# A Mamba and LoRA layer on one core: ScalarE takes B's rows out of PSUM, transposed tiles get two buffers, and the LoRA factor's product is made ahead of condition 1

## The chip, the cores and the metric

The kernel runs on 1 core of one Trainium2 chip. The metric is the device time of one execution in microseconds (us). An execution under the profiler is also taken; its span runs from the first to the last instruction. The engines are TensorE (PE; PEld is its weight load), VectorE (DVE), ScalarE (ACT), GpSimd (POOL) and SyncE (SP, which only issues DMAs here). Each works through its own instructions strictly in the order in which the program gives them.

## The reference

```python
# x: (32, 64, 1024) fp32
def cond(x, ids, W, A, B):            # LoRA of rank 16, adapter chosen per batch
    return x @ W + (x @ A[ids]) @ B[ids]
def attn(x, A_log, D, x_proj_w, dt_proj_w, dt_proj_b):      # selective scan, 16 states
    A = -exp(A_log)
    xp = x @ x_proj_w.T               # 32 columns dt_in, 16 columns B, 16 columns C
    dt = softplus(dt_in @ dt_proj_w.T + dt_proj_b)
    dA = exp(dt[..., None] * A)
    dBx = dt[..., None] * B[:, :, None, :] * x[..., None]
    h_t = dA_t * h_{t-1} + dBx_t      # over 64 steps; y_t = sum over n of h_t * C_t
    return y + D * x
x = x + attn(cond(x, ids1, W, A, B), ...)
x = x + ffn(cond2(x, ids2, ...), ...)  # a second LoRA layer, then 4 gated low-rank experts
```

## The kernel before

**Tiling.** The 32 batches are worked in 8 groups G of 4 (T = 256 tokens). The 1024 channels are 8 blocks j of 128 partitions. For each block the 16 states are worked in 4 units un (8 states of 2 batches: 1024 columns), so a group has 32 steps (j, un), the whole kernel 256. In each step

- TensorE makes dBx of the unit (`b_times_dtx`, 4 matmuls of `stacked` with the diagonal matrices `Bd`, into one of two PSUM tiles dBx0 and dBx1),
- VectorE runs the scan h = dA * h + dBx (line 1009), 1024 columns,
- GpSimd multiplies h by C into `hC` (line 578),
- TensorE, three steps later (LAG = 3), adds up the states by 8 transposing matmuls into yp[j % 2] (`sum_states`, line 1212),
- ScalarE makes dA, the exponentials of dt * A, for a later step (`decays`, line 612).

**Jobs.** All other work is put between the steps by a table written out by hand: `JOBS[(j, un)]` is a list of `job(name, i, bank, ks, ahead)`. FIRST, SIXTH and FINAL are the tables of group 0, of the last group but one and of the last; SIXTH is JOBS without the jobs for two groups on (xT, GAs, xr and the early parts of cond). The bank says which PSUM tile the job's product goes to: "A" is jb[0], "B" is jb[1], "Y" is yp[j % 2], which `sum_states` of block j writes from step (j, 3) on. Before TensorE writes a bank it waits until the bank's last tenant is released (`tenant`, `released`). TensorE does `b_times_dtx`, then `sum_states`, then the jobs of the step. VectorE does the jobs of a step after its scan; those in LATE_ON_DVE (dtz, cond and others), and on ScalarE those in LATE_ON_ACT (stack, Bst, xT, dtz and others), one step later.

The jobs around the change:

- `xT` i (0 to 3): x of a later group, transposed. ScalarE copies the high part (line 641), VectorE makes the low part (line 907).
- `GAs`, `xr`: the LoRA factor A split in high and low, and its product with xT (16 matmuls of 256 columns). VectorE masks it into `low` (line 911).
- `cond` i: 24 matmuls of W with xT for the channels of block i, then 1 with `low` and the LoRA factor B. Of the work ahead, cond 0 and the first eighth of cond 1 are made in the group before.
- `xproj`, then `dtz` i: dt before softplus; three operations of ScalarE (lines 593 to 597), one of VectorE (line 811), for blocks 2i and 2i + 1; dtz 4 and 5 are those of the next group.
- `Bst`: B's rows, transposed three times over onto 96 partitions (line 1145). Before, ScalarE makes the high part of rows 64 to 95 (line 660), VectorE writes the low part back to the same PSUM bank (line 921). From that bank VectorE makes the four diagonals `Bd` (`b_diagonals`, line 826), placed by `DIAGONALS`: 0, 1 and 2 at (7, 0), (7, 1), (7, 3) for the next group, 3 at (0, 1). The bank is released by the fourth. PE's `b_times_dtx` waits for its diagonal where j is 0.
- `stack` i: GpSimd multiplies dt by u into `dtx` (line 558, placed by `DTX`), TensorE transposes it, ScalarE makes the high half of `HL` (line 637), VectorE the low half (line 903), SP writes HL to HBM (`put_dtx`) and reads it back in another layout (`stack_dtx`) as `stacked`. stack 8 and 9 are blocks 0 and 1 of the next group. dtx and HL have one buffer each: GpSimd waits for the transpose before it, ScalarE for the DMA that reads HL.

`add_residual` (line 817) stands on VectorE before the scan at un = 3.

**Set-up.** Before group 0, W is split into high and low parts piece by piece: ScalarE `W_high(o)`, VectorE `W_low(o)` (line 949), and `put_W(o)` writes the pair to HBM. TensorE transposes xproj's and dtproj's weights, makes the first seven eighths of cond 0 and of cond 1, then xr, then the rest of both, then cond 2 to 7, xproj and what the first scan needs. ScalarE's order is: xprojT (line 703), dtprojT (lines 706, 709), GAs, put_W 0 and 1, W_high 2, put_W 2, W_high 3, put_W 3. VectorE's is: dtprojT (line 959), GAs, W_low 2, W_low 3, then `low`.

## Time and profile before

| | us |
|---|---|
| median of 3 runs | 902.66 (901.97 to 914.94) |
| the profiled execution | 902.51 |
| its span, first to last instruction | 900.7 |
| TensorE busy | 810.4 (90%) |
| VectorE busy | 761.5 (85%) |
| GpSimd busy | 661.1 (73%) |
| ScalarE busy | 639.3 (71%) |
| scans (line 1009), 256 | 582.7 |
| multiplications by C (line 578), 256 | 612.7 |
| mean granted clock of TensorE | 0.963 of full speed |

Busy time is an average over the stages. The granted clock has two levels, 1.0 (2.4 GHz) and 0.5 (1.2 GHz). A row of the timeline gives the start, the time from the first start to the last end of the instructions merged in it, their number, and in brackets how long the engine was idle before and what ended that. Matmuls of one engine overlap, so a row of TensorE may start before the row above it has ended.

### The profile page before, as it was taken

What the parts mean: (1) busy time and instruction counts of PE and PEld (TensorE: products, weight loads), DVE (VectorE), ACT (ScalarE), POOL (GpSimd) and SP (SyncE); (2) the same over time, 40 slices, a digit from 0 to 9 for tenths busy, and PEclk for the clock granted to TensorE, in tenths of its full rate; (3) what the DMA queues carried; (4) which work ended last, traced back from release to release, by engine and by line L of the source; (5) the groups of instructions that cost most, each with busy time, mean ns of one, the idle gap of its engine ahead of it and who ended that gap; (6) DMA issues with size and microseconds to landing.
All of it is one profiled execution on the core that took longest, in us unless ns stands there. A gap on an engine that the chain in (4) does not pass through costs nothing.

```text
span 900.7 us, 18606 instructions
## 1 busy us (share of the span) xinstructions
PE 810.4 (90%) x6416; PEld 773.0 (86%) x6416; DVE 761.5 (85%) x688; ACT 639.3 (71%) x1481; POOL 661.1 (73%) x349
## 2 busy tenths in 40 slices
PE   5898999899989999899989998899998999778884
PEld 4898999799978998799988997889988999677772
DVE  2437789988998899988999896998999979999993
ACT  4547677788776877777786875778777867779750
POOL 2004878689877888688877885779876978889891
PEclk9996999999999999899999998999999999899998
DMA  9988688375557557475666755476674744253221
GB/s 245 376 325 270 207 260 229 135 234 187 188 178 249 191 159 239 160 251 153 209 196 206 225 166 190 128 251 200 192 226 136 243 149 147 84 164 101 88 65 47
DMA packets 103113, 172.24 MB, mean 191 GB/s; under 512 B 21865, under 2 KB 71657, under 8 KB 94830
## 3 DMA queue, kind: packets, MB, share of 16 engines
q1 hardware_dynamic: 85614, 94.12, 35.0%
q10 hardware_dynamic: 17408, 76.95, 24.4%
q8 instruction: 53, 0.87, 0.4%
q14 instruction: 38, 0.31, 0.1%
HBM read 137.33 MB, written 33.69 MB: 190 GB/s over the span
## 4 chain that ended last, share of the span: by engine, by line
PE 60%; DVE 15%; ACT 8%; issue 6%; POOL 6%; DMA 3%; SPq 1%; ACTq 0%; POOLq 0%; DVEq 0%
PE jb L1045 26%; PE yp L1212 17%; DVE h L1009 10%; PE dBx L1045 8%; POOL hC L578 5%; ACT dA L612 3%; PE yp L1045 3%; PE jb L1049 3%; PE yp L1049 2%; DVE HL L903 1%; DVE Bd L826 1%; DMA x<-in_x 1%; DMA GA<-in_L_cond_lora_B_w 1%; PE yp L1217 1%; DMA stacked<-dtx_scratch 1%
## 5 line engine op out<-in xcount | busy, mean ns | idle before, releaser
L578 POOL TENSOR_TENSOR hC<-h,Cb 128x1024 f32<-128x1024 f32 (+1 forms) x256 | 612.7, 2395 | 161.2 <-DVE h L1009 144.8
L1009 DVE TENSOR_TENSOR_SCAN h<-dA,dBx 128x1024 f32<-128x1024 f32 x256 | 582.7, 2279 | 50.3 <-PE dBx L1045 40.4
L612 ACT ACTIVATE dA<-dt,negA 128x252 f32<-128x252 f32 x1024 | 430.3, 494 | 67.5 <-DVE h L1009 57.3
L1212 PE MATMUL yp<-ident,hC 128*128 128x128 f32 x2048 | 277.9, 280 | 27.7 <-DVE xT L907 11.3
L1212 PEld LDWEIGHTS yp<-ident,hC 128*128 128x128 f32 x2048 | 238.9, 145 | 33.6 <-issue 28.1
L1045 PE MATMUL jb<-xT,Wst 128*128 128x256 f32 x1416 | 213.9, 293 | 0.0
L1045 PE MATMUL dBx<-Bd,stacked 96*128 96x256 f32 x1024 | 187.6, 306 | 10.4 <-DVE h L1009 5.2
L1045 PEld LDWEIGHTS jb<-xT,Wst 128*128 128x128 f32 x1416 | 183.7, 192 | 1.9
L1045 PEld LDWEIGHTS dBx<-Bd,stacked 96*128 96x128 f32 x1024 | 147.5, 196 | 15.9 <-issue 12.8
L558 POOL TENSOR_TENSOR dtx<-dt,u 128x256 f32<-128x256 f32 x64 | 47.2, 738 | 44.4 <-DVE dt L811 42.4
L637 ACT ACTIVATE HL<-yp 128x256 fp32r<-128x256 f32 x54 | 20.4, 377 | 42.6 <-PE yp L1049 40.3
L647 ACT ACTIVATE u<-jb 128x512 f32<-128x512 f32 x31 | 18.6, 598 | 39.3 <-PE jb L1045 36.9
L1045 PE MATMUL jb<-low,GB 128*128 128x256 f32 x128 | 38.3, 380 | 2.3 <-DVE low L911 2.3
L1049 PE MATMUL yp<-ident,dtx 128*128 128x128 f32 x108 | 21.7, 284 | 18.9 <-DVE dt L811 11.7
L826 DVE TENSOR_TENSOR Bd<-jb,diag 96x1024 fp32r<-96x1024 f32 x32 | 38.2, 1197 | 0.1
L903 DVE TENSOR_TENSOR HL<-yp,HL 128x256 fp32r<-128x256 f32 x54 | 22.4, 414 | 16.7 <-ACT HL L637 16.5
L1217 PE MATMUL yp<-ident,Du 128*128 128x128 f32 x128 | 35.0, 274 | 0.0
L1045 PE MATMUL jb<-G,x1T 128*128 128x132 f32 x256 | 33.7, 279 | 1.0 <-ACT x1T L639 0.7
L1049 PEld LDWEIGHTS yp<-ident,dtx 128*128 128x128 f32 x108 | 13.5, 145 | 22.9 <-DVE dt L811 14.3
L639 ACT ACTIVATE x1T<-jb 128x512 f32<-128x512 f32 x32 | 19.0, 594 | 19.7 <-PE jb L1049 19.4
L1045 PEld LDWEIGHTS jb<-G,x1T 128*128 128x128 f32 x256 | 30.8, 190 | 1.8 <-ACT x1T L639 0.9
L603 ACT ACTIVATE Du<-u,Dsb 128x256 f32<-128x256 f32 x64 | 31.6, 495 | 0.0
(170 smaller groups left out, 729.4 us busy)
## 6 DMA issues: line engine op xcount, KB each, us to landing
...
```

Source lines behind the costliest of these rows:

```text
L558: pool.tensor_tensor(dtx[:, :], dt[:, i % NDT, :], u[:, i % K, :], ALU.mult).then_inc(dtx_made, 1)
L578: pool.tensor_tensor(*(x[:, :, ns, :] for x in times_C(un)), ALU.mult).then_inc(hC_made, 1)
L603: act.activation(Du[:, i % 4, :], u[:, i % K, :], ACT.Copy, scale=Dsb[:, i % K:i % K + 1]).then_inc(Du_made, 1)
L612: act.activation(dA[:, half % NDA, :].rearrange("p (b n t) -> p b n t", b=GB_, n=HS)[:, :, n, 1:STEPS], dt[:, j % NDT, :].rearrange("p (b ...
L637: act.activation(HL[:, 0, :, :].rearrange("p q d -> p (q d)"), psum[:, 0:2 * P], ACT.Copy).then_inc(hi_made, 1)
L826: dve.tensor_tensor(Bd[0:ROWS, NQ // 2 * p:NQ // 2 * (p + 1), HS * half:HS * (half + 1), :], rows[:, NQ // 2 * p:NQ // 2 * (p + 1), HS * h ...
L903: dve.tensor_tensor(HL[:, 1, :, :].rearrange("p q d -> p (q d)"), psum[:, 0:2 * P], HL[:, 0, :, :].bitcast(fp32).rearrange("p q d -> p (q ...
L1009: dve.tensor_tensor_scan(h[:, un % NH, :], dA[:, half % NDA, UNIT * p:UNIT * (p + 1)], dBx[un % 2][:, :], 0.0, ALU.mult, ALU.add).then_inc ...
L1045: return pe.matmul(o, lhsT, rhs, start=start, stop=stop, **kw)
L1049: return pe.matmul(o, in_, ident[first:first + n, first:first + n], is_transpose=True, start=True, stop=True)
L1212: last = pe.matmul(y, hC[:, un % NHC, P * n:P * (n + 1)], ident[:, :], is_transpose=True, start=un == 0 and n == 0, stop=False, skip_group ...
L1217: last = pe.matmul(y, Du[:, j % 4, P * p:P * (p + 1)], ident[:, :], is_transpose=True, start=False, stop=True, skip_group_check=True)
```

## The change

Tables: at (6, 2) Bst goes to "Y" and xT 3 to "B". stack 8 and 9 go to "B". The first three eighths of cond 0 move from (7, 0), where they stood ahead of stack 8, to (7, 1). Diagonal 0 of the next group moves from (7, 0) to (6, 3). FIRST gets the same edits.

Bst: ScalarE copies all 96 rows, rounded, into Bhl, and rows 64 to 95 once more, unrounded, into the new tile B_raw; that releases the bank. VectorE makes the low part from B_raw and Bhl, and the diagonals from Bhl, all in SBUF. Since diagonal 0 is now made before the group's last block has used the old one, b_diagonals waits for dBx_full.

Buffers: dtx and HL get two buffers, and what waited for the last use now waits for the last but one. The DMA scratch of GpSimd, which issues no DMA here, is cut to make room.

Set-up: on TensorE xr moves between the first parts of cond 0 and cond 1, to another PSUM bank; on ScalarE GAs, W_high 2, put_W 0 and 1 and W_high 3 move ahead of dtprojT; on VectorE GAs, W_low 2, W_low 3 and `low` do.

```diff
@@ JOBS and FIRST
-    (6, 2): [job("Bst", 0, "B"), job("xT", 3, "Y"), job("dtz", 4, "A")],
+    (6, 2): [job("Bst", 0, "Y"), job("xT", 3, "B"), job("dtz", 4, "A")],
     (6, 3): [],
-    (7, 0): [job("xr", 0, "Y", (0, 4)), job("xr", 0, "Y", (4, 8)), job("cond", 0, "A", (0, 3), 2), job("stack", 8, "Y")],
-    (7, 1): [job("cond", 0, "A", (3, 4), 2), job("dtz", 5, "Y")],
-    (7, 2): [job("cond", 0, "A", (4, 8), 2), job("stack", 9, "Y")],
+    (7, 0): [job("xr", 0, "Y", (0, 4)), job("xr", 0, "Y", (4, 8)), job("stack", 8, "B")],
+    (7, 1): [job("cond", 0, "A", (0, 4), 2), job("dtz", 5, "Y")],
+    (7, 2): [job("cond", 0, "A", (4, 8), 2), job("stack", 9, "B")],
@@
-DIAGONALS = {(0, 1): 3, (7, 0): 0, (7, 1): 1, (7, 3): 2}
+DIAGONALS = {(0, 1): 3, (6, 3): 0, (7, 1): 1, (7, 3): 2}
@@ buffers
+        B_raw = sb("B_raw", [P, NQ, R])
-        dtx = sb("dtx", [P, T])
+        dtx = sb("dtx", [P, 2, T])
-        HL = sb("HL", [P, 2, 2, P], fr)
+        HL = sb("HL", [P, 2, 2, 2, P], fr)
@@ GpSimd, make_dtx
-                wait(pool, full["stack"], K * G + i)
+                wait(pool, full["stack"], K * G + i - 1)
@@ ScalarE, stack
-                    wait(act, HL_out, 16 * (K * g + i))
+                    wait(act, HL_out, 16 * (K * g + i - 1))
@@ ScalarE, Bst
-                    wait(act, b_step, 2 * g)
-                    act.activation(Bhl[2 * Q:ROWS, :, :]..., psum[2 * Q:ROWS, 0:NQ * R], ACT.Copy).then_inc(b_step, 1)
+                    wait(act, Bd_made, UNITS * g)
+                    wait(act, b_low, g)
+                    act.activation(Bhl[0:ROWS, :, :]..., psum[0:ROWS, 0:NQ * R], ACT.Copy).then_inc(b_rows, 1)
+                    act.activation(B_raw[2 * Q:ROWS, :, :]..., psum[2 * Q:ROWS, 0:NQ * R], ACT.Copy).then_inc(b_rows, 1)
@@ ScalarE, set-up
+            job("GAs", 0, 0, None)
+            W_high(2)
+            put_W(0)
+            put_W(1)
+            W_high(3)
             for i in range(2):
                 ...
-            job("GAs", 0, 0, None)
-            put_W(0)
-            put_W(1)
-            W_high(2)
             put_W(2)
-            W_high(3)
             put_W(3)
@@ VectorE, b_diagonals
-                dve.wait_ge(b_step, 2 * G + 2)
+                dve.wait_ge(b_low, G + 1)
+                if G:
+                    dve.wait_ge(dBx_full, UNITS * (K * G - 1) + un + 1)
@@ VectorE, Bst
-                    low_rows = psum[2 * Q:ROWS, 0:NQ * R]
-                    dve.tensor_tensor(low_rows, low_rows, Bhl[2 * Q:ROWS, :, :]..., ALU.subtract).then_inc(b_step, 1)
+                    low_rows = Bhl[2 * Q:ROWS, :, :]
+                    dve.tensor_tensor(low_rows, B_raw[2 * Q:ROWS, :, :], low_rows.bitcast(fp32), ALU.subtract).then_inc(b_low, 1)
@@ VectorE, set-up
+            job("GAs", 0, 0, 0, None)
+            W_low(2)
+            W_low(3)
+            job("xr", 0, 0, 0, set_bank(3))
             for i in range(2):
                 ...
-            job("GAs", 0, 0, 0, None)
-            W_low(2)
-            W_low(3)
-            job("xr", 0, 0, 0, set_bank(4))
@@ TensorE, released
                 if name == "Bst":
-                    return Bd_made, UNITS * g + UNITS
+                    return b_rows, 2 * g + 2
@@ TensorE, set-up
             job("cond", 0, 0, 0, jb[0], "A", (0, K - 1))
             pe.wait_ge(taken["xT"], 4)
+            job("xr", 0, 0, 0, set_bank(3), None)
             job("cond", 1, 0, 0, jb[1], "B", (0, K - 1))
             wait(pe, set_taken, 1)
-            job("xr", 0, 0, 0, set_bank(4), None)
@@
-    nc = _bacc.Bacc("TRN2", target_bir_lowering=False, num_devices=1)
+    nc = _bacc.Bacc("TRN2", target_bir_lowering=False, num_devices=1, dynamic_dma_scratch_size=1024)
```

## Rows read from the trace of the kernel before

**Rows 1.** Busy time by stage, cut at scan starts; the first line names the columns.

```profile
core 0: us, PE busy (x) PEld busy (x) DVE busy (x) ACT busy (x) POOL busy (x), PEclk, DMA share, GB/s
72.20:180.18 107.98, 101.72 (x785) 99.49 (x785) 90.32 (x68) 77.19 (x182) 81.23 (x40) 0.92 0.71 221
384.41:464.50 80.09, 78.77 (x656) 75.92 (x654) 72.52 (x66) 61.43 (x145) 66.28 (x33) 1.00 0.63 205
464.50:487.07 22.57, 18.37 (x138) 17.62 (x139) 20.50 (x20) 15.96 (x38) 15.99 (x9) 0.92 0.54 170
773.25:794.40 21.15, 13.79 (x84) 12.87 (x83) 19.70 (x18) 16.10 (x38) 16.47 (x9) 0.76 0.31 97
```

**Rows 2.** Timeline, VectorE in group 3's boundary: start, us, engine, operation, idle before.

```profile
468.08 2.28 DVE L1009 TENSOR_TENSOR_SCAN h<-dA,dBx 128x1024 f32<-128x1024 f32 x1
470.28 0.67 DVE L811 SCALAR_TENSOR_TENSOR dt<-jb,dt 128x512 f32<-128x512 f32 x1
470.86 2.28 DVE L1009 TENSOR_TENSOR_SCAN h<-dA,dBx 128x1024 f32<-128x1024 f32 x1
473.05 1.19 DVE L826 TENSOR_TENSOR Bd<-jb,diag 96x1024 fp32r<-96x1024 f32 x1
...
475.64 0.42 DVE L903 TENSOR_TENSOR HL<-yp,HL 128x256 fp32r<-128x256 f32 x1 [1.06 <-ACT HL L637]
475.98 2.28 DVE L1009 TENSOR_TENSOR_SCAN h<-dA,dBx 128x1024 f32<-128x1024 f32 x1
...
483.09 0.42 DVE L903 TENSOR_TENSOR HL<-yp,HL 128x256 fp32r<-128x256 f32 x1 [0.94 <-ACT HL L637]
```

**Rows 3.** Timeline, TensorE in the same boundary.

```profile
464.64 0.75 PE L1049 MATMUL yp<-ident,xin 128*128 128x128 f32 x4 [0.30 <-DVE xT L907]
...
467.98 1.07 PE L1212 MATMUL yp<-ident,hC 128*128 128x128 f32 x8 [1.88 <-DVE xT L907]
...
471.04 2.84 PE L1045 MATMUL yp<-xT,GAs 128*128 128x256 f32 x16
...
474.80 0.38 PE L1049 MATMUL yp<-ident,dtx 128*128 128x128 f32 x2
...
482.20 0.44 PE L1049 MATMUL yp<-ident,dtx 128*128 128x128 f32 x2 [1.63 <-DVE dt L811]
...
483.66 1.06 PE L1212 MATMUL yp<-ident,hC 128*128 128x128 f32 x8 [0.56 <-DVE HL L903]
```

**Rows 4.** Timeline, TensorE's stack 8 in group 1's boundary.

```profile
269.26 0.44 PE L1049 MATMUL yp<-ident,dtx 128*128 128x128 f32 x2 [1.24 <-DVE low L911]
```

**Rows 5.** Timeline of the set-up, TensorE and ScalarE.

```profile
17.73 7.13 PE L1045 MATMUL jb<-xT,Bd 128*128 128x256 f32 x42 [1.10 <-DVE Bd L949]
...
18.29 0.60 ACT L703 ACTIVATE xprojT<-dBx 128x512 f32<-128x512 f32 x1 [1.00 <-issue]
...
25.14 2.14 PE L1045 MATMUL dBx<-xT,GAs 128*128 128x256 f32 x16 [0.28 <-DVE GAs L896]
...
29.91 0.70 PE L1045 MATMUL jb<-low,GB 128*128 128x256 f32 x2 [2.27 <-DVE low L911]
```

**Rows 6.** Busy time by stage, the 3.41 us after the 1.88 us wait.

```profile
469.21:472.62 3.41, 3.41 (x18) 3.41 (x17) 3.41 (x3) 2.77 (x7) 2.21 (x2) 0.50 0.01 3
```

**Rows 7.** Set-up: a stage by busy time, and SP's first put_dtx in the timeline.

```profile
63.00:65.00 2.00, 2.00 (x21) 2.00 (x20) 0.96 (x2) 0.63 (x2) 0.58 (x1) 1.00 0.06 14
...
65.30 0.36 SPq L421 DMA_DIRECT2D dtx_scratch<-HL  x1
```

**Rows 8.** Timeline, VectorE: 512 elements from PSUM, and from SBUF.

```profile
467.14 0.69 DVE L907 TENSOR_TENSOR xT<-yp,xT 128x512 fp32r<-128x512 f32 x1
...
17.50 0.68 DVE L949 TENSOR_TENSOR Bd<-Cb,Bd 128x512 fp32r<-128x512 f32 x1
```

**Rows 9.** Timeline of the boundary, ScalarE's copy of Bst and GpSimd's dtx 8.

```profile
465.60 0.27 ACT L660 ACTIVATE Bhl<-jb 32x128 fp32r<-32x128 f32 x1
...
472.79 0.74 POOL L558 TENSOR_TENSOR dtx<-dt,u 128x256 f32<-128x256 f32 x1
```

More of the change, by code:

```diff
@@ L102 @@
     (6, 1): [job("xT", 2, "Y")],
-    (6, 2): [job("Bst", 0, "B"), job("xT", 3, "Y"), job("dtz", 4, "A")],
+    (6, 2): [job("Bst", 0, "Y"), job("xT", 3, "B"), job("dtz", 4, "A")],
     (6, 3): [],
-    (7, 0): [job("xr", 0, "Y", (0, 4)), job("xr", 0, "Y", (4, 8)), job("cond", 0, "A", (0, 3), 2), job("stack", 8, "Y")],
-    (7, 1): [job("cond", 0, "A", (3, 4), 2), job("dtz", 5, "Y")],
-    (7, 2): [job("cond", 0, "A", (4, 8), 2), job("stack", 9, "Y")],
+    (7, 0): [job("xr", 0, "Y", (0, 4)), job("xr", 0, "Y", (4, 8)), job("stack", 8, "B")],
+    (7, 1): [job("cond", 0, "A", (0, 4), 2), job("dtz", 5, "Y")],
+    (7, 2): [job("cond", 0, "A", (4, 8), 2), job("stack", 9, "B")],
     (7, 3): [job("cond", 1, "A", (0, 1), 2)],
@@ L122 @@
 DU = {(0, 1): 2, (1, 3): 3, (2, 3): 4, (3, 1): 5, (4, 0): 6, (5, 0): 7, (6, 3): 8, (7, 1): 9}
-BANK_OF_B = next(q[2] for at in JOBS for q in JOBS[at] if q[0] == "Bst")
 LORA_A, LORA2, LORA_B, LORA2_B = range(4)
 ADAPTERS = {(1, 2): LORA2_B, (3, 0): 0, (4, 0): 1, (5, 2): 2}
-DIAGONALS = {(0, 1): 3, (7, 0): 0, (7, 1): 1, (7, 3): 2}
+DIAGONALS = {(0, 1): 3, (6, 3): 0, (7, 1): 1, (7, 3): 2}
 def layer_kernel(nc, x, ids1, ids2, W, loraA, loraB, A_log, Dw, xproj_w, dtproj_w, dtproj_b,
@@ L269, in layer_kernel @@
         last_half = sem("last_half_of_hC")
[L270 removed]
+        bc_made, b_rows, b_low, Bd_made = map(sem, ["bc_made", "b_rows", "b_low", "Bd_made"])
         gate_step, gate_exp, gm_hi, expB_put, expB_hi = map(sem, ["gate_step", "gate_exp", "gm_hi", "expB_put", "expB_hi"])
@@ L556, in make_dtx @@
                 pool.wait_ge(taken["dtz"], K // 2 * G + i // 2 + 1)
-                wait(pool, full["stack"], K * G + i)
-                pool.tensor_tensor(dtx[:, :], dt[:, i % NDT, :], u[:, i % K, :], ALU.mult).then_inc(dtx_made, 1)
+                wait(pool, full["stack"], K * G + i - 1)
+                pool.tensor_tensor(dtx[:, i % 2, :], dt[:, i % NDT, :], u[:, i % K, :], ALU.mult).then_inc(dtx_made, 1)
             pool.wait_ge(s_expB, 64)
@@ L658, in job @@
                 elif name == "Bst":
-                    wait(act, b_step, 2 * g)
-                    act.activation(Bhl[2 * Q:ROWS, :, :].rearrange("p q n -> p (q n)"), psum[2 * Q:ROWS, 0:NQ * R], ACT.Copy).then_inc(b_step, 1)
+                    wait(act, Bd_made, UNITS * g)
+                    wait(act, b_low, g)
+                    act.activation(Bhl[0:ROWS, :, :].rearrange("p q n -> p (q n)"), psum[0:ROWS, 0:NQ * R], ACT.Copy).then_inc(b_rows, 1)
+                    act.activation(B_raw[2 * Q:ROWS, :, :].rearrange("p q n -> p (q n)"), psum[2 * Q:ROWS, 0:NQ * R], ACT.Copy).then_inc(b_rows, 1)
                 elif name == "A2T":
@@ L820, in b_diagonals @@
             def b_diagonals(G, un):
-                dve.wait_ge(b_step, 2 * G + 2)
+                dve.wait_ge(b_low, G + 1)
+                if G:
+                    dve.wait_ge(dBx_full, UNITS * (K * G - 1) + un + 1)
                 half, p = un // 2, un % 2
                 of = [ROWS, NQ // 2, HS, Q]
-                rows = jb["AB".index(BANK_OF_B) if G else 0][0:ROWS, 0:NQ * R].rearrange("p (q n) -> p q n", q=NQ)
                 dve.tensor_tensor(
                     Bd[0:ROWS, NQ // 2 * p:NQ // 2 * (p + 1), HS * half:HS * (half + 1), :],
-                    rows[:, NQ // 2 * p:NQ // 2 * (p + 1), HS * half:HS * (half + 1)].unsqueeze(3).to_broadcast(of),
+                    Bhl[0:ROWS, NQ // 2 * p:NQ // 2 * (p + 1), HS * half:HS * (half + 1)].bitcast(fp32).unsqueeze(3).to_broadcast(of),
                     diag[0:ROWS, :].unsqueeze(1).unsqueeze(1).to_broadcast(of), ALU.mult).then_inc(Bd_made, 1)
@@ L902, in job @@
                     dve.wait_ge(hi_made, K * g + i + 1)
-                    dve.tensor_tensor(HL[:, 1, :, :].rearrange("p q d -> p (q d)"), psum[:, 0:2 * P],
-                                      HL[:, 0, :, :].bitcast(fp32).rearrange("p q d -> p (q d)"), ALU.subtract).then_inc(taken[name], 1)
+                    dve.tensor_tensor(HL[:, i % 2, 1, :, :].rearrange("p q d -> p (q d)"), psum[:, 0:2 * P],
+                                      HL[:, i % 2, 0, :, :].bitcast(fp32).rearrange("p q d -> p (q d)"), ALU.subtract).then_inc(taken[name], 1)
                 elif name == "xT":
@@ L1010, in body @@
                                                0.0, ALU.mult, ALU.add).then_inc(h_made, 1)
-                        if j == K - 1 and (j, un) in DIAGONALS and not final:
+                        if j >= K - 2 and (j, un) in DIAGONALS and not final:
                             b_diagonals(G + 1, DIAGONALS[j, un])
@@ L1100, in job @@
                     for a in range(2):
-                        last = tr(psum[:, P * a:P * (a + 1)], dtx[:, P * a:P * (a + 1)], P)
+                        last = tr(psum[:, P * a:P * (a + 1)], dtx[:, i % 2, P * a:P * (a + 1)], P)
                 elif name == "x1T":
@@ L1258, in _ @@
                         for a in range(4):
-                            last = tr(set_bank(3 + i)[:, n * a:n * (a + 1)], F_n[:, :].rearrange("m (p k) -> m k p", k=K)[:, 4 * i + a, :], n)
+                            last = tr(set_bank(4 - i)[:, n * a:n * (a + 1)], F_n[:, :].rearrange("m (p k) -> m k p", k=K)[:, 4 * i + a, :], n)
                         last.then_inc(set_full, 1)
```

11 lines of the change are left out of this document (4 added, 7 removed).

## The prediction

> **What bounds the kernel now.** I read the profile in four steps.
>
> First, the busy time by stage, cut at the starts of scans [rows 1]. The kernel is 72.2 us of set-up, eight groups of 32 scans and a tail. Group 0 takes 108.0 us, group 3 takes 80.09 + 22.57 = 102.7. Group 3 splits in two. In its body, from its first scan to scan (6,2), TensorE is busy 78.77 of 80.09 us: the body runs at TensorE's pace. In what I call the boundary, from scan (6,2) to the next group's first scan, TensorE is busy 18.37 of 22.57 us and VectorE 20.50: no engine is full, something waits. The change works in this stretch and in the set-up.
>
> Second, the timeline of VectorE and TensorE through that boundary [rows 2, 3]. TensorE waits four times: 1.88 us for DVE's low part of xT 3, because sum_states(6,0) writes yp[0], which xT 3 holds; 1.63 for DVE's dt, because stack 9 goes to yp[1], held by dtz 5; 0.56 for the low part of stack 9, before sum_states(7,0); 0.30 for xT 2. VectorE waits twice, each time for ScalarE's half of HL: 1.06 and 0.94 us. Stack 8 is late because the first cond 0 matmuls and xr stand ahead of it; it also shares yp[1] with xr, and in group 1, where TensorE's clock was full, it waits 1.24 for DVE's low of xr [rows 4].
>
> Third, the set-up [rows 5]. xr stands behind the first parts of both cond 0 and cond 1, and TensorE then waits 2.27 us for low (plus 0.28 before xr), because VectorE makes two pieces of W first. From there to the first scan TensorE and the chain of small operations have hardly a gap.
>
> Fourth, the granted clock [rows 6]: 0.50 in the 3.41 us after the 1.88 wait, that is 1.2 GHz instead of 2.4. The 16 matmuls of xr took 2.84 us there [rows 3] and 2.14 in the set-up at full clock [rows 5].
>
> **The change part by part.** The sum is made against the profiled execution, 902.51 us (span 900.7 and 1.8 around it); the median of the runs is 902.66, so the two may be used alike.
>
> *Set-up.* The first 42 matmuls of cond 0 and cond 1 take 7.13 us [rows 5], so after cond 0's 21 TensorE is at 17.73 + 3.57 = 21.3. xr needs GA_split. GAs now follows xprojT, whose copy ends at 18.9: 0.6 on ScalarE (a copy of that size) and 0.7 on VectorE [rows 5, 8], ready at 20.2. xr runs 21.3 to 23.45, cond 1 to 27.0. VectorE then makes W 2 and W 3 (two operations of 0.7 each, behind two copies of 0.6), low at about 24.2 to 24.6: before 27.0, so neither wait is left. Gain 0.28 + 2.27 = 2.55. dtprojT moves behind W 3 on ScalarE; nobody needs it before dtz 0, after the whole of cond. Of the DMAs on ScalarE's queue W_scratch 0 and 1 are issued 1.5 us earlier, 2 and 3 within a microsecond of before; their landing is awaited by W 5 to 7, a dozen microseconds later. W pieces 4 to 7 keep their distance to TensorE. What could eat the gain is the DMA, which moves the same bytes in either order: its share is 0.06 from 63 us on; put_dtx(0,0) was issued at 65.30, and would now go at 62.8, before that lull [rows 7]. On SP's queue nothing else changes place. I take 2.5, bounds 1.0 and 2.6. The F transposes swap two banks, at no cost.
>
> *Bst by ScalarE.* Added: ScalarE copies 96 rows instead of 32, and makes one more copy of 32. The copy of 32 rows and 128 columns took 0.27 [rows 9], one of 128 rows and 512 columns 0.60 [rows 5]: 0.27 to 0.60 each, and I take 0.27, so 0.27 more per group, ahead of xT 3's copy on an engine busy 15.96 of 22.57 us [rows 1]. dtz 4 follows 0.3 to 0.45 later, still ahead of VectorE. VectorE's low part and the four diagonals (1.19 each [rows 2]) read SBUF instead of PSUM. The same operation on 512 elements takes 0.69 from PSUM and 0.68 from SBUF [rows 8], so I price that at nothing; bounds 0 and 0.1 each. The Trainium skill, page VectorE: DVE Perf Modes, section on the TRN2 errata, gives PSUM sources 62 cycles more fixed cost than SBUF ones. By it each diagonal is 0.065 us cheaper and the sum some 1.5 us lower; the rows do not show such a difference.
>
> *Banks at (6,2).* Bst now waits for xT 2 where xT 3 did: 0.75 us of wait instead of 0.30. xT 3 in jb[1] no longer holds yp[0]; sum_states(6,0) needs only ScalarE's two copies, at about 466.15. TensorE is there at 466.45 instead of 467.98. dBx(7,0) is done at 468, so the new wait of diagonal 0 (dBx_full) costs nothing: VectorE comes to it at 470.3.
>
> *(6,3) to (7,3) on VectorE.* From start to start [rows 2] a scan takes 2.2, a diagonal 1.12, dt 0.58, HL 0.34; low and residual, of HL's size, are taken like it. Scan (6,3) at 468.08 as before. Diagonal 0 now follows it, dt at 471.4, scan (7,0) at 472.0: 1.1 late. Stack 8 needs dtx 8, which GpSimd makes behind hC(6,3), at 472.79 to 473.53 as before [rows 9]; dt at 472.05 is in time. xr ends at about 470.9, cond 0's nine matmuls no longer stand in between, so TensorE idles 2.7 us to 473.55 and issues stack 8 then instead of 474.80. ScalarE's HL is done at 474.35, VectorE has low at 474.2 and HL at 474.5, with no wait: scan (7,1) at 474.85, was 475.98. Diagonal 1, scan (7,2) at 478.2 (TensorE's dBx for it, with 12 matmuls of cond ahead, full at 477.5). Stack 9 in jb[1] no longer waits for dtz 5: TensorE reaches it at 480.4, was 482.20. dt, HL (wait 0.15), residual, scan (7,3) at 481.9, diagonal 2, next group's first scan at 485.2, was 487.07. So the boundary costs VectorE's own 20.50 and 0.15: gain 1.9. The second buffers of dtx and HL are what lets stack 8 and 9 follow so closely; elsewhere I price them at nothing, since none of the waits above is for the old buffer. Of what queues behind the new waits: behind Bst on TensorE stand xT 3 and dtz 4, half a microsecond late with slack on both.
>
> *The body after it* is TensorE's, which reaches sum_states(7,0) at about 481.2 instead of 483.66, so it keeps the 1.9. Against that stands the clock: a 2.7 us gap is longer than the 1.88 that was followed by half clock, and TensorE's work from stack 8 to stack 9 (6.85 us) now lies on the path. One half-speed stretch there costs up to 1.7 us of TensorE, 0.9 of it past VectorE's slack. One boundary in three: 0.3 each. The present stretch is hidden: at full clock the same stack 8 waited 1.24 us instead [rows 4]. The choice is mine, between 0 and 1.7.
>
> Sum: 2.5 set-up; six boundaries by 1.9 - 0.3 = 1.6, that is 9.6; the last boundary (no xT, xr, cond) can give its idle VectorE time, 21.15 - 19.70 = 1.45 [rows 1], taken as 1.3. Together 13.4: 902.5 - 13.4 = **889**.
>
> The Trainium skill, page TensorE: Matmul & The Clock Gate, section What's actually happening, says that activity releases the throttle and idleness brings it back; this trace agrees (0.50 after the wait), and it is what speaks against a longer single gap.
>
> **The rivals.**
> (a) TensorE keeps more than VectorE's 1.9: it enters each group 2.4 us earlier and loses less to its slow stretch, and the body follows it. For: the body's 98%. Against: GpSimd, busy 66.28 + 15.99 = 82.3 us a group [rows 1], has to follow. 2.6 a boundary: 2.5 + 15.6 + 1.4 = 19.5, 883.
> (b) The boundary gives nothing: the wait for dtx 8 and one half-speed stretch in each boundary hold stack 9 at 482. For: the present gaps are already followed by a slow stretch [rows 6]. Only the set-up and 0.3 a boundary: 898.
> (c) Slower: the clock stays at 1.2 GHz over all of stack 8 to stack 9. 6.85 us of work then end at 480.4 + 3.4 = 483.8, 1.6 later than stack 9 now. It decides from more than one stretch of 3.4 us per boundary on. Longer stretches exist: group 0's mean granted clock is 0.92 [rows 1], that is 17 of its 108 us at 0.5. In every boundary: 902.5 - 2.5 + 6 x 1.6 = 909.6.
>
> **How the numbers follow.** The forecast 0.52, (a) 0.26, (b) 0.17, (c) 0.05. The forecast's own range is 885 to 894. The range to hold the time 8 times in 10 reaches into (a) and (b): 879 to 899, with the DMA bound of the set-up (1.5) and the price of half clock (up to 1.7 a boundary) inside it. 2% below the median is 884.6, about what a measurement of this kernel can tell from no change: (a) lies beyond it, the tip of the forecast too; faster 0.27, within 2% 0.70, slower 0.03.
>
> **What would show it.** Right: no wait over 1 us between xr and the F transposes in the set-up, first scan at 69.7; sum_states at (6,3) without a wait for xT; stack 8 waiting for GpSimd's dtx instead; HL's waits on VectorE gone; boundary 20.6 to 21. Wrong: first scan after 71; a boundary above 22; granted clock 0.5 between stack 8 and stack 9 in most groups; GpSimd's waits for scans shrinking in the body, which is rival (a).

## The result, and the profile after

The changed kernel takes 911.42 us (median of 4 runs, 908.23 to 912.86) where the kernel before took 902.32 beside it: ratio 1.0114, interval 1.0062 to 1.0166. The forecast was 889, 1.5% faster; it became 1.1% slower, outside the range of 879 to 899. A second series has 911.93 against 910.13 for the kernel before (ratio 1.0039, 0.9996 to 1.0081): the loss is between nothing and 1.7%, and the 13 us of gain are in neither series.

The profiled execution: 908.23 us, span 906.0. Stages cut as in [rows 1]; then a window of 3.40 us.

```profile
388.54:467.99 79.45, 76.13 (x628) 73.10 (x626) 72.33 (x67) 61.75 (x145) 68.10 (x33) 1.00 0.65 210
467.99:491.28 23.29, 19.60 (x154) 19.12 (x155) 20.58 (x20) 16.18 (x39) 17.85 (x9) 0.93 0.49 153
478.93:482.33 3.40, 3.40 (x19) 3.40 (x18) 3.40 (x3) 1.85 (x5) 2.74 (x3) 0.50 0.21 77
```

The boundary of group 3 takes 23.29 us (before 22.57, forecast 20.7), and the new thing in it is GpSimd: busy 17.85 us for the nine operations that took 15.99. The costliest groups of instructions say the same of the whole run:

```profile
L578 POOL TENSOR_TENSOR hC<-h,Cb 128x1024 f32<-128x1024 f32 (+1 forms) x256 | 632.5, 2475 | 145.0 <-DVE h L1011 130.6
L558 POOL TENSOR_TENSOR dtx<-dt,u 128x256 f32<-128x256 f32 x64 | 54.2, 847 | 39.2 <-DVE dt L813 39.2
L829 DVE TENSOR_TENSOR Bd<-Bhl,diag 96x1024 fp32r<-96x1024 f32 x32 | 38.6, 1208 | 0.1
L1051 PE MATMUL jb<-ident,dtx 128*128 128x128 f32 x48 | 9.7, 284 | 26.0 <-POOL dtx L558 26.0
```

Before, the 256 hC took 612.7 us (mean 2395 ns) and the 64 dtx 47.2 (738 ns). On GpSimd only dtx was edited, its buffer index and what it waits for, and GpSimd works 27 us longer. The diagonals themselves have not changed (1208 ns, before 1197). The timeline of the boundary on VectorE and GpSimd, to be held against [rows 2, 9]:

```profile
471.55 2.28 DVE L1011 TENSOR_TENSOR_SCAN h<-dA,dBx 128x1024 f32<-128x1024 f32 x1
473.74 1.19 DVE L829 TENSOR_TENSOR Bd<-Bhl,diag 96x1024 fp32r<-96x1024 f32 x1
474.86 0.68 DVE L813 SCALAR_TENSOR_TENSOR dt<-jb,dt 128x512 f32<-128x512 f32 x1
475.46 2.27 DVE L1011 TENSOR_TENSOR_SCAN h<-dA,dBx 128x1024 f32<-128x1024 f32 x1
477.65 0.40 DVE L914 TENSOR_TENSOR low<-yp,own_batch 128x256 f32<-128x256 f32 x1
478.83 0.42 DVE L906 TENSOR_TENSOR HL<-jb,HL 128x256 fp32r<-128x256 f32 x1 [0.79 <-ACT HL L637]
...
473.91 3.24 POOL L578 TENSOR_TENSOR hC<-h,Cb 128x1024 f32<-128x1024 f32 x1 [1.06 <-DVE h L1011]
477.11 0.71 POOL L558 TENSOR_TENSOR dtx<-dt,u 128x256 f32<-128x256 f32 x1
...
495.99 1.73 POOL L558 TENSOR_TENSOR dtx<-dt,u 128x256 f32<-128x256 f32 x1
```

Diagonal 0 starts at 473.74, the hC beside it at 473.91, and that one takes 3.24 us instead of 2.4; dtx 8 waits behind it. In the next group's (0, 1), diagonal 3 starts at 495.94, just ahead of dtx 2, which takes 1.73 us instead of 0.74.

The last boundary takes 23.45 us, where it took 21.15. There Bst's low part, which now also reads two inputs from SBUF, started 0.02 us behind an hC and ended 0.15 us after it, having taken 2.53 us where it takes 0.28 in the other seven groups:

```profile
776.98 2.40 POOL L578 TENSOR_TENSOR hC<-h,Cb 128x1024 f32<-128x1024 f32 x1
777.00 2.53 DVE L924 TENSOR_TENSOR Bhl<-B_raw,Bhl 32x128 fp32r<-32x128 f32 x1 [0.23 <-ACT B_raw L662]
```

TensorE in the boundary of group 3, the counterpart of [rows 3]:

```profile
468.37 0.52 PE L1147 MATMUL yp<-ident,x1T 16*96 16x16 f32 x8 [1.03 <-DVE xT L910]
...
472.86 2.15 PE L1047 MATMUL yp<-xT,GAs 128*128 128x256 f32 x16
477.97 0.41 PE L1051 MATMUL jb<-ident,dtx 128*128 128x128 f32 x2 [2.96 <-POOL dtx L558]
478.14 0.72 PE L1047 MATMUL dBx<-Bd,stacked 96*128 96x256 f32 x4
478.70 1.69 PE L1214 MATMUL yp<-ident,hC 128*128 128x128 f32 x8
480.25 2.60 PE L1047 MATMUL jb<-xT,Wst 128*128 128x256 f32 x12
```

The 1.88 us wait for xT 3 is gone, as forecast, and one of 2.96 us for dtx 8 stands in its place. Behind it the clock is at 0.50: twelve matmuls of cond 0 take 2.60 us, which take 1.67 elsewhere.

### The profile page after: what moved, and what is told of

Its sections match the earlier page's. It is cut to its first block, busy times and chain, and to the rows that moved or that the text cites. A ratio compares the mean times of both kernels' runs of the same rounds, so it can differ in the third digit from the quotient of the medians.

```text
span 906.0 us, 18640 instructions
## 1 busy us (share of the span) xinstructions
PE 806.1 (89%) x6416; PEld 770.7 (85%) x6416; DVE 764.7 (84%) x688; ACT 643.4 (71%) x1489; POOL 688.2 (76%) x349
## 4 chain that ended last, share of the span: by engine, by line
PE 52%; POOL 12%; DVE 11%; issue 10%; ACT 9%; DMA 5%; SPq 0%; POOLq 0%; ACTq 0%; DVEq 0%
PE jb L1047 24%; PE yp L1214 13%; POOL hC L578 10%; PE dBx L1047 7%; DVE h L1011 6%; ACT dA L612 4%; PE jb L1051 3%; PE yp L1047 3%; DMA Cb<-c_scratch 2%; POOL dtx L558 2%; DMA dtx_scratch<-HL 1%; DVE Bd L829 1%; DMA x<-in_x 1%; PE yp L1051 1%; PE yp L1219 1%
## 5 line engine op out<-in xcount | busy, mean ns | idle before, releaser
L578 POOL TENSOR_TENSOR hC<-h,Cb 128x1024 f32<-128x1024 f32 (+1 forms) x256 | 632.5, 2475 | 145.0 <-DVE h L1011 130.6
L1214 PE MATMUL yp<-ident,hC 128*128 128x128 f32 x2048 | 274.7, 278 | 16.7 <-DVE HL L906 8.0
L1214 PEld LDWEIGHTS yp<-ident,hC 128*128 128x128 f32 x2048 | 236.7, 144 | 20.7 <-issue 11.4
L1047 PEld LDWEIGHTS jb<-xT,Wst 128*128 128x128 f32 x1416 | 186.2, 195 | 1.9
L558 POOL TENSOR_TENSOR dtx<-dt,u 128x256 f32<-128x256 f32 x64 | 54.2, 847 | 39.2 <-DVE dt L813 39.2
L829 DVE TENSOR_TENSOR Bd<-Bhl,diag 96x1024 fp32r<-96x1024 f32 x32 | 38.6, 1208 | 0.1
L910 DVE TENSOR_TENSOR xT<-jb,xT 128x512 fp32r<-128x512 f32 x26 | 17.8, 684 | 21.3 <-ACT xT L641 21.1
L639 ACT ACTIVATE x1T<-jb 128x512 f32<-128x512 f32 x32 | 19.1, 596 | 22.4 <-PE jb L1051 21.7
L641 ACT ACTIVATE xT<-jb 128x512 fp32r<-128x512 f32 x26 | 15.5, 596 | 26.8 <-PE jb L1051 26.2
L1051 PE MATMUL jb<-ident,dtx 128*128 128x128 f32 x48 | 9.7, 284 | 26.0 <-POOL dtx L558 26.0
L1047 PE MATMUL jb<-u,xprojT 128*128 128x256 f32 x128 | 30.5, 381 | 0.7 <-ACT u L647 0.7
```

The lines of the kernel that those rows point to most:

```text
L558: pool.tensor_tensor(dtx[:, i % 2, :], dt[:, i % NDT, :], u[:, i % K, :], ALU.mult).then_inc(dtx_made, 1)
L578: pool.tensor_tensor(*(x[:, :, ns, :] for x in times_C(un)), ALU.mult).then_inc(hC_made, 1)
L639: act.activation(x1T[:, 2 * i:2 * i + 2, :].rearrange("p k t -> p (k t)"), psum[:, :], ACT.Copy).then_inc(taken[name], 1)
L829: dve.tensor_tensor(Bd[0:ROWS, NQ // 2 * p:NQ // 2 * (p + 1), HS * half:HS * (half + 1), :], Bhl[0:ROWS, NQ // 2 * p:NQ // 2 * (p + 1), HS ...
L1047: return pe.matmul(o, lhsT, rhs, start=start, stop=stop, **kw)
L1051: return pe.matmul(o, in_, ident[first:first + n, first:first + n], is_transpose=True, start=True, stop=True)
```

## The experiments

Two causes are to be told apart, and each may have a share. **P**: a VectorE operation with two inputs in SBUF lengthens the GpSimd operation beside it. **C**: TensorE's wait for dtx 8 is followed by 1.2 GHz in a place where that counts. Each span is taken apart into the start of the first scan, the seven boundaries, the eight bodies and a tail of 36.0 us, the same in both. All ratios and intervals are against runs of the kernel before on the same chip. There it took 906.8 to 911.9 us, not the 902 from which the expected times were worked out, so it is the ratios that are compared.

| | first scan | sum of the boundaries | sum of the bodies | hC over 2.7 us |
|---|---|---|---|---|
| before | 72.2 | 156.4 | 636.1 | 7 |
| changed | 69.3 | 163.7 | 637.0 | 29 |

The sums of the bodies are not alike inside: before's hold some 6 us in group 4, where TensorE waits 3.2 us for a transfer of stacked. The shortest bodies take 78.7 us before, and 79.45 changed (three groups).

**Set-up alone.** The kernel before, with the hunks of the set-up only.

> The kernel before with the set-up part of the change alone. Theory P (the two engines GpSimd and VectorE hold each other up where both read SBUF) and theory C (TensorE's clock falls after the longer wait for dtx 8) both say that the loss lies in the boundary edits and not here: first scan at 69.3 us as in the changed kernel instead of 72.2, everything else as before, 899.5 us, ratio 0.997. A rival, that the moved set-up is what upsets the later phase of clock and DMAs, would give a time above before's, 905 or more.

906.93, ratio 0.9965 (0.9915 to 1.0015). First scan at 70.0; the boundaries take 156.5, as before. The set-up is not the cause.

**Old tables with the new copy of B, the masking left out, and condition 1 first.** Three edits of the changed kernel: the tables and diagonal 0 as before; the diagonals as an operation with one input; only the order in (7, 0) to (7, 1) as before.

```
-                    ... diag[0:ROWS, :].unsqueeze(1).unsqueeze(1).to_broadcast(of), ALU.mult)
+                dve.tensor_scalar(..., 1.0, None, ALU.mult)
```

> The changed kernel with the tables of before (banks, cond 0 ahead of stack 8, diagonal 0 at (7, 0)): what is left is the set-up, the second buffers, and Bst copied out by ScalarE with the diagonals read from SBUF. Theory P: each diagonal makes GpSimd's operation beside it about 0.9 us longer (3.24 instead of 2.37 us in the changed kernel), so GpSimd stays at 686 us busy instead of 661, and the time is 3 to 8 us above that of the set-up alone, 903 to 908. Theory C: the clock has nothing to do with it, TensorE's waits are those of before, and the time is that of the set-up alone, 899.5, with GpSimd at 661.

> The changed kernel, in which the diagonals are made as a copy of the same shape with one input from SBUF (times 1.0) instead of a product of two: the masking of Bd is left out, the rest is the same work. If the copy takes the same 1.2 us on VectorE, theory P says that GpSimd's operations beside it are 2.4 us again, its busy time 661, dtx 8 is 0.9 us earlier, the boundary of group 3 falls from 23.3 to about 21.5 to 22.5 and the time by 6 to 10 us to 902 to 905. Theory C says no change, 911, since the wait for dtx 8 stays over 2 us long.

> The changed kernel with the first three eighths of cond 0 back ahead of stack 8 in (7, 0). They fill TensorE's wait for dtx 8 (2.96 us in group 3) with 1.25 us of work. Theory C: the clock keeps 1.0 between stack 8 and stack 9, the 1.03 us wait of scan (7, 2) for dBx goes, the time falls by 6 x 1 to 2 us, to 900 to 905. Theory P: GpSimd's operations beside the diagonals stay 3.2 us, dtx 8 comes when it came, and the time falls by 3 us at most, to 908 or more.

910.48 (ratio 1.0017, 0.9969 to 1.0065), 898.0 (0.9940, 0.9895 to 0.9986) and 907.2 (0.9998, 0.9955 to 1.0040). With the old tables 29 hC over 2.7 us stay and the boundaries take 161.9 instead of the 156.5 of the set-up alone: the longer operations come with the copy of B, not with the table. In time the two kernels cannot be told apart, for their intervals overlap.

With condition 1 first the boundaries take 156.8, 6.9 less than changed, as C had it, and 29 hC stay long, as P had it; neither expectation holds whole, and three of the first six boundaries still have a half-clock stretch at (7, 0). (Its bodies sum to 646.2, but this profile is of the longest of its ten executions, 913.83 us, so nothing is read from that.)

The run with one input is not the clean control that it was meant to be, for that operation takes 0.66 us instead of 1.19, and hC beside it 2.71 to 2.78. Three of its seven boundaries take 20.65 to 20.71 us, the forecast's figure, but VectorE is busy only 18.98 us there instead of 20.5, so they are not the forecast's chain. What it does show is the price of half clock. The stages (boundary of group 3, of group 4, and a stretch of the latter):

```profile
460.14:480.80 20.66, 17.26 (x150) 16.99 (x151) 18.98 (x19) 15.63 (x37) 16.25 (x9) 1.00 0.46 125
563.76:585.98 22.22, 18.83 (x150) 18.56 (x151) 18.97 (x19) 15.61 (x37) 16.27 (x9) 0.92 0.43 139
573.75:577.15 3.40, 3.40 (x18) 3.40 (x18) 3.08 (x3) 2.27 (x6) 2.74 (x3) 0.50 0.21 77
```

The engines do the same work in both boundaries and TensorE waits 3.01 us for dtx 8 in both; only the second has the half-clock stretch, and it is 1.56 us longer. So such a wait is not always followed by half clock: of five boundaries of this run with the 3.01 us wait, three have the stretch.

**One operand back in PSUM.** The changed kernel; the second factor of each diagonal is read from dBx in PSUM instead of diag in SBUF (same shape, wrong factor from group 1 on). Beside it the same with condition 1 first, the changed kernel again, and one with dtz 4 and dtx 8 a step sooner.

```
-                    diag[0:ROWS, :].unsqueeze(1).unsqueeze(1).to_broadcast(of), ALU.mult)
+                    dBx[(s + 1) % 2][0:ROWS, :].rearrange("p (q n t) -> p q n t", ...), ALU.mult)
```

> The changed kernel, in which from group 1 on the second factor of the diagonals is read from PSUM (the next unit's dBx) instead of from diag in SBUF: the values of Bd are wrong, the operation, its shape and its 1.2 us are the same, and only one input lies in SBUF. Port theory: GpSimd's multiplications beside it are 2.4 us again (busy 663 instead of 688), dtx after diagonal 3 is 0.74 instead of 1.7 us, each boundary falls by 0.9 us at least to 22.4 where the clock still falls and to 20.7 to 21 where it does not; time 6 to 9 us below the changed kernel's. If two inputs in SBUF are not what matters (but the longer chain, or the clock alone), GpSimd stays at 688 and nothing moves.

> Both suspected causes taken away: the second factor from PSUM as in the run before, and the first three eighths of cond 0 back ahead of stack 8, to fill the wait for dtx 8. If port and clock together are the whole loss, most boundaries are 20.7 to 21.2 us, the forecast's, no boundary is above 22.5, and the time is 12 to 16 us below the changed kernel's, about 889 to 893 where before takes 902. If something else is lost as well, boundaries stay above 22.

> The changed kernel itself beside the next three on one chip. Both theories take its boundary of 23.3 us as 20.7 as forecast, 0.9 for GpSimd's longer operation ahead of dtx 8 (port) and 1.6 for TensorE at half clock afterwards. Expected: boundaries of 23.3 us again, 28 or 29 of GpSimd's multiplications over 2.7 us, one slow stretch after nearly every wait for dtx 8, time 5 us above before's.

> The changed kernel with dtz 4 moved from (6, 2) to (6, 1), behind xT 2, and dtx 8 made by GpSimd after hC(6, 2) instead of hC(6, 3). dtx 8 is then done some 3 us before TensorE comes to stack 8, so its wait of 3 us and the slow stretch after it should go (clock theory: boundaries of 20.6 to 21.5 us, time 10 to 14 us below the changed kernel's). The diagonals still read two inputs from SBUF: GpSimd's busy time stays at 688 (port theory), but ahead of dtx 8 it costs nothing now. If the longer operations of GpSimd hold up the scans themselves, boundaries stay at 22 or more.

897.06 (0.9876, 0.9795 to 0.9958), 898.72 (0.9846, 0.9762 to 0.9930), 911.93, and 907.74 (0.9979, 0.9932 to 1.0025). Where one operand lies changes 15 us, more than the 6 to 9 expected. GpSimd is busy 664.4 us instead of 688.2, and 7 hC are over 2.7 us as before the change. Two lines of its profile page, then a diagonal and the hC beside it, 0.16 us behind it as in the changed kernel:

```profile
PE 804.2 (90%) x6416; PEld 767.4 (86%) x6416; DVE 762.7 (86%) x688; ACT 641.6 (72%) x1489; POOL 664.4 (75%) x349
...
L834 DVE TENSOR_TENSOR Bd<-Bhl,dBx 96x1024 fp32r<-96x1024 f32 x28 | 33.7, 1203 | 13.0 <-PE dBx L1052 13.0
```
```profile
276.33 1.19 DVE L834 TENSOR_TENSOR Bd<-Bhl,dBx 96x1024 fp32r<-96x1024 f32 x1
276.49 2.43 POOL L578 TENSOR_TENSOR hC<-h,Cb 128x1024 f32<-128x1024 f32 x1 [1.05 <-PE yp L1219]
```

P is shown: same operation, same duration, same moment, and hC takes 2.43 us instead of 3.24 to 3.31. The boundaries of this run take 21.2 and 21.4 us without a half-clock stretch at (7, 0) and 22.7 with one (behind waits for dtx 8 of 2.67 us; the waits of 1.42 and 1.79 had none), though its diagonals wait 13.0 us for dBx, which they did not before. The last takes 23.09, for the low part still reads two inputs from SBUF. With condition 1 first as well, four boundaries take 20.4 us, but three take 24 to 26, where none was expected above 22.5. The changed kernel again has 28 hC over 2.7 us and three boundaries of 23.3, others from 22.3 to 24.6; it lies 1.8 us above before's median there, where 5 were expected.

The kernel before had the effect too. All of its seven hC over 2.7 us start 0.16 us behind a VectorE operation with two inputs in SBUF:

```profile
447.26 0.67 DVE L896 TENSOR_TENSOR GAs<-GA,GAs 128x512 fp32r<-128x512 f32 x1
447.42 2.75 POOL L578 TENSOR_TENSOR hC<-h,Cb 128x1024 f32<-128x1024 f32 x1 [0.37 <-DVE h L1009]
```

In the last run dtx 8 starts at 474.60 and TensorE finds it ready, with no half-clock stretch at (7, 0), yet the boundaries take 22.4 us, where C expected 20.6 to 21.5. For the move pushed Bst's low part beside an hC, and there is the same effect the other way round:

```profile
472.28 2.38 POOL L578 TENSOR_TENSOR hC<-h,Cb 128x1024 f32<-128x1024 f32 x1 [0.64 <-DVE h L1011]
473.17 1.64 DVE L924 TENSOR_TENSOR Bhl<-B_raw,Bhl 32x128 fp32r<-32x128 f32 x1 [0.38 <-ACT B_raw L662]
```

VectorE's operation takes 0.28 us elsewhere; here it starts inside an hC and ends 0.15 us after it. It does so in each of the first six boundaries, and scan (6, 3) starts 5.84 us after scan (6, 2) instead of 3.56; of these 2.3 us the low part's delay is 1.4, the rest dt, which now stands ahead of it, and the 0.38 us wait.

**B's rows kept in PSUM, with the rest of the change but one swap.** Bst goes to the last 128 columns of jb[1], whose first 256 take stack 8 and 9, and stays there, so diagonals and low part read PSUM. For that xT 3 goes to yp[0] again, as before the change. Then the same with 12 matmuls of no use ahead of stack 8, the same with condition 1 first, and the changed kernel with 20 such matmuls.

```
+        def b_in(g):
+            return jb[1][:, 512 - NQ * R:512] if g else jb[0][:, 0:NQ * R]
...
+                    if i == K:
+                        for k in range(FILLERS):
+                            mm(psum[:, 0:T], GAs[...], xT[:, 0, k % K, :], True, True)
                     pe.wait_ge(dtx_made, K * g + i + 1)
```

> The changed kernel with B's rows left in PSUM as before (in the last 128 columns of the bank that LoRA's products 8 and 9 use in their first 256, instead of being copied out by ScalarE), so that each diagonal has one operand in PSUM again. Set-up, two buffers of HL and dtx, stack 8 ahead of condition 1 and diagonal 0 at (6, 3) stay as changed. Nothing is left out. Theory P (a VectorE operation with two inputs in SBUF lengthens the GpSimd operation beside it by 0.9 us): GpSimd busy 664 us instead of 688, no hC over 2.7 us in the boundaries, boundaries of 21.2 us without and 22.7 with a half-clock stretch (23.3 in the changed kernel), the stretch (0, 0) to (6, 2) 78.6 us instead of 79.5, in all as the run with the other factor in PSUM: ratio 0.985 to 0.991, 897 to 902 us. Rival (the 15 us came from Bst leaving its bank and ScalarE's copy, or from the values of Bd that the run with the other factor had wrong): ratio 1.00 or more.

> g1_rows_kept, and 12 matmuls of no use (128x256, into the bank of LoRA's product 8, overwritten by it) put into TensorE's wait for dtx 8, which was 1.8 us in the run with the other factor in PSUM. Nothing is left out. Theory C (TensorE's wait is what the half-clock stretch at (7, 0) follows): the stretches at (7, 0) go in most of the seven boundaries, these take 21.2 us instead of 22.7, five of 1.5 us make 7.5 us: ratio to before 0.977 to 0.984. Rival (the stretch comes whatever TensorE does there, from the busy share of the whole boundary or from a wait elsewhere such as the 1.04 us for xT at (6, 2)): stretches and boundaries as in g1_rows_kept, within 2 us of it.

> g1_rows_kept, and condition 1's first matmuls ahead of LoRA's product 8 in (7, 0), as before the change. Nothing is left out. If the order of these two is worth what the forecast had (TensorE idles while condition 1 could run): 2 us less in each boundary with stack 8 first, so this kernel 8 to 14 us slower than g1_rows_kept. If it is worth nothing, as the runs with the other factor in PSUM have it (897.1 and 898.7 us): within 3 us of g1_rows_kept, four boundaries of 20.4 us and some of 24 to 26 with a half-clock stretch of 6.8 us in condition 1.

> The changed kernel, and 20 matmuls of no use (128x256, 2.8 us at full clock) in TensorE's wait for dtx 8, which is 3.0 us there. Nothing is left out. Theory C: half-clock stretches at (7, 0) go, boundaries of 21.7 us instead of 23.3, so 8 to 11 us less than the changed kernel: ratio to before 0.992 to 0.998. Rival (clock falls anyway, or the fillers run at half clock and hold stack 8 up): boundaries 23.3 or more, ratio 1.004 or more.

898.15 (0.9889, 0.9813 to 0.9966), 904.51 (0.9933, 0.9886 to 0.9980), 904.91 (0.9943, 0.9896 to 0.9991), 906.91 (0.9975, 0.9938 to 1.0012). The boundary of the first and a stretch of it, by busy time; then the timeline of its GpSimd and TensorE there:

```profile
461.61:482.62 21.01, 18.44 (x141) 17.82 (x142) 20.43 (x19) 16.08 (x38) 16.04 (x9) 0.92 0.52 138
464.59:467.99 3.40, 2.90 (x14) 2.93 (x15) 2.88 (x3) 3.19 (x9) 2.18 (x2) 0.50 0.44 148
```
```profile
467.55 2.40 POOL L580 TENSOR_TENSOR hC<-h,Cb 128x1024 f32<-128x1024 f32 x1 [1.22 <-DVE h L1012]
469.94 0.74 POOL L560 TENSOR_TENSOR dtx<-dt,u 128x256 f32<-128x256 f32 x1
470.83 0.41 PE L1052 MATMUL jb<-ident,dtx 128*128 128x128 f32 x2
```

Boundaries of 20.9 to 21.0 us (one of 23.2, with a wait of 3.29 us for a transfer of stacked; the last 20.4), near the forecast's 20.7 with VectorE's whole work, so its chain was about right without P. A half-clock stretch is in this one too, but right behind the wait for xT 3, which this kernel keeps, and there it costs 0.1 us: the boundary of group 4, which has none, takes 20.89. Stack 8 follows xr without a wait in the row above (only in group 4 does it wait, 1.37 us), so the fillers had no gap to fill: they ran 1.6 us, held stack 8 up by 1.4, and the boundaries take 22.4. Theory C's expectation for this kernel failed, for it rested on a wait that is not there. In the changed kernel, where the wait is, they did what C said; its boundary by busy time, and TensorE's timeline:

```profile
465.57:487.28 21.71, 20.32 (x173) 19.79 (x174) 20.49 (x19) 16.17 (x39) 17.91 (x9) 1.00 0.53 165
```
```profile
471.96 2.56 PE L1047 MATMUL jb<-xT,GAs 128*128 128x256 f32 x20
475.52 0.44 PE L1051 MATMUL jb<-ident,dtx 128*128 128x128 f32 x2 [1.01 <-POOL dtx L558]
```

In the first six boundaries no half-clock stretch is left at (7, 0); five of the six take 21.7 to 22.0 us (expected were 21.7) instead of 23.3. The sixth takes 23.97, with a wait of 3.82 us for a transfer of stacked at (7, 3); the last still takes 23.46, with its low part at 2.53 us. GpSimd's 17.91 us show that P is still there.

**Again, and the order alone.** The kernel with B's rows kept once more; and the kernel before with only stack 8 ahead of cond 0.

```
-    (7, 0): [..., job("cond", 0, "A", (0, 3), 2), job("stack", 8, "Y")],
+    (7, 0): [..., job("stack", 8, "Y"), job("cond", 0, "A", (0, 3), 2)],
```

> g1_rows_kept once more, with more rounds: its four runs had a median of 898.2 us and a ratio of 0.981 to 0.997, while the same kernel with condition 1 first had 904.9 us in ten runs. Theory P: boundaries of 21.0 us where no half-clock stretch lies behind (7, 0), six times 1.5 us less than before, 3 us less in the set-up and nothing elsewhere: ratio 0.985 to 0.991. Rival (the four runs were lucky ones, and the gain is that of the set-up with half of the boundaries' lost again in the groups' other steps): 0.993 to 0.997.

> The kernel before, and of the change only the order of two entries of the table: LoRA's product 8 ahead of condition 1's first matmuls in (7, 0), still in the bank that it had. Nothing is left out. Theory O (the order is what the forecast had the gain from: 1.2 us of product 8, given back to scan (7, 1)): boundaries of 21.3 us instead of 22.57, 7 us in all, ratio 0.990 to 0.994. Theory B (the gain comes from the two buffers, the bank of product 8 and diagonal 0 at (6, 3), and the order is worth nothing, as boundaries of 21.0 us with product 8 first and 20.5 to 21.5 with condition 1 first have it): boundaries of 22.3 to 22.6 us, ratio 0.998 to 1.002.

895.75 (0.9807, 0.9747 to 0.9867; a little more than P's 0.985 to 0.991), and 908.33 (0.9952, 0.9909 to 0.9994). The order alone makes the boundary longer, 23.25 us, which neither theory had:

```profile
478.43 0.44 PE L1049 MATMUL yp<-ident,dtx 128*128 128x128 f32 x2 [2.33 <-DVE low L911]
```

Stack 8 in yp[1] waits for low, and cond 0 stands behind it. With the new bank and buffers the order makes no difference to the boundaries (148.4 us in all with stack 8 first, 148.8 with condition 1 first). So the boundaries' gain comes from the bank of stack 8 and 9, the two buffers and diagonal 0 at (6, 3) together; which of the three was not separated. In time, 904.91 us with condition 1 first lies 6.8 above the 898.15 beside it, between the two expectations, with overlapping intervals; what the order is worth elsewhere stays open. That the order alone still had a ratio just below 1 is not explained by its profile.

**Where the rest went.** The kept rows give 8.0 us in the boundaries, but GpSimd then waits in the next group's first steps for C's rows. GpSimd's wait for them in the second profile of the kept rows (us in total, times, longest), and the same row of the kernel before:

```profile
POOL hC L580 <- DMA Cb<-c_scratch: 16.5, 5, 4.0
```
```profile
POOL hC L578 <- DMA Cb<-c_scratch: 5.3, 4, 2.0
```

The last experiment puts the load of C's third part ahead of stack_dtx on SP's queue at (7, 3); beside it the kept rows a third time.

```
+                        c_first = (j, un) == (K - 1, UNITS - 1) and not last
+                        if c_first:
+                            spread_c(G + 1, un - 1)
                         for name, i, g, gpar, psum in ended_before(G, par, j, un):
```

> g1_rows_kept, and on SP's queue at (7, 3) the load of C's third part ahead of the loads of LoRA's product 9 (stack_dtx), whose wait for the write of HL held it for 5 us. Nothing is left out. Theory: the boundary's gain is in part given back because GpSimd waits for C's rows in the next group's (0, 2) or (0, 3) (16.5 us in five waits in g1_rows_kept's second profile, 5.3 us in the kernel before), so issued 4 us sooner the third part lands before it is wanted and the fourth no later: the first four scans of a group take 11.3 to 12.5 us instead of 14.5 to 14.9, the whole group 1.1 us less, 7 times: ratio 0.970 to 0.982. Rival (the transfers share the DMA engines with those of product 9 and the bytes of the conditions' weights, so C's fourth part is as late as before, and product 9 later): as g1_rows_kept, within 2 us.

> g1_rows_kept a third time, on the chip of the run with C's rows sooner, to compare the two: ratio 0.981 to 0.989, the middle of its intervals so far.

893.59 (0.9854, 0.9815 to 0.9894) and 894.61 (0.9888, 0.9834 to 0.9942). The first four scans of groups 1, 2, 3 and 5 take 11.3 us as expected (14.1 to 14.9 in most groups without it), so in these steps the queue's order was the wait. GpSimd still waits 11.1 us for C's rows in all, where the three profiles of the kept rows have 14.1 to 21.1. The whole is 1 us shorter, which these runs cannot tell from nothing, and the ratio misses the expected 0.970 to 0.982: in its profile group 0 lost 7 us at another place and group 4 another 4.

## Why the prediction was wrong

**The set-up**: the waits were right, the size is not shown. xr follows cond 0 without a wait, and low is ready in time. The first profile has the first scan at 69.29 (forecast 69.7), a gain of 2.9. But that is in part the luck of two profiles: in the 16 profiles with the new set-up the first scan starts at 69.3 to 72.4 us, half of them below 70.3, and in the two with the old one at 72.20 and, in the run of the order alone, at 70.62. Its ratio alone, 0.9965, does not exclude 1.

**The low part and the diagonals from SBUF, priced at nothing**: this step failed, and with it "dtx 8 as before". The 0.69 against 0.68 of [rows 8] is true of VectorE's own time, and 1208 against 1197 ns confirms it. What was not asked is who else works then. Each diagonal starts just ahead of an operation of GpSimd, and each lengthens one: 22 hC by 0.9 us more than before, and seven dtx by 1.0 (one of them in the set-up). In the boundary that puts dtx 8 at 477.11, 5.56 us after the start of scan (6, 3), where it was 4.71. Its price is the step from the kept rows' 20.9 to 21.0 us to the 21.7 with fillers and no half clock, 0.7 to 0.8. In the body it is diagonal 3 beside dtx 2: 79.45 us in the shortest bodies where it was 78.7, an estimated 5 us over seven groups, which the forecast did not have at all. The kernel before already showed the effect, in the seven hC beside GAs, but only in GpSimd's rows.

The Trainium skill has the rule, page SBUF — State Buffer, section Who interferes with whom: a VectorE instruction with two SBUF inputs contends with a GpSimd instruction that reads SBUF, since its second input comes through the shared read interface. The runs agree: with one operand in PSUM the prolongation is gone. The Trainium skill, same page, section Summary: rules for kernel authors, says that the second to issue fully blocks until the first finishes. That agrees nearly: hC behind diagonal 0 would end at 474.93 + 2.38 = 477.31 by it, and ended at 477.15; the low part behind an hC ended 0.15 us after it.

**The price of half clock**: mis-sized. The forecast had 0.3 a boundary, from one in three. The changed kernel has one in five of the first six boundaries, starting 0.2 to 1.3 us after stack 8, behind waits of 2.96 to 3.56 us for dtx 8, and there it costs 1.56 (one input) to 1.6 (fillers). The sixth, that of group 1, waited 1.99 us and has none there; it takes 23.70 us with a wait of 3.53 at (7, 3). The forecast had 1.7 as a bound and let half of it vanish in VectorE's slack. Its observation that the old stretch is hidden was right, and it holds for the kept rows too. The kept rows' 20.9 to 21.0, with 0.7 to 0.8 for P and 1.6 for the clock, make the measured 23.3. That sum closes in part by construction, since P's and the clock's terms meet at the run with fillers; the independent check is the 1.56 of the run with one input.

**The VectorE chain**: about right. Boundaries of 20.9 to 21.0 with the kept rows, which do VectorE's whole work, stand against the forecast's 20.65. HL's waits are not gone in the changed kernel (0.79 at 478.83), since stack 8 is late.

**The wait for xT 3**: right; it is gone, and sum_states(6, 0) follows the dBx before it without one. Bst waits 1.03 us for xT 2 where 0.75 was forecast.

**The last boundary**: wrong, 23.45 instead of 19.85. It is the same cause at another operation: the low part takes 2.53 us instead of 0.28, and scan (6, 3) starts 5.40 us after scan (6, 2), where the kernel before has 2.97. The run with the other factor in PSUM, whose low part is as late, keeps 23.09; with the low part reading PSUM (the kept rows) it is 20.4.

**The rivals**: (c), 909.6, had the sign and nearly the size at a chance of 0.05, and the clock is half of its mechanism; but it wanted more than one stretch per boundary, and one suffices once GpSimd is late too. Rival (b) named the wait for dtx 8 with one stretch in each boundary, held to the old place of stack 9. No rival had GpSimd slower, which is the term that turned the sign. The gain of 13.4 us was not far off once the operand stays in PSUM (ratios 0.981 to 0.989 are 10 to 17 us), but by other terms than the sum's: 8.0 in the boundaries instead of 10.9, and less in the set-up.
